# Two VectorE operands into PSUM, a reordered slot, and a convolution folded into TensorE's weights, in a two-layer Mamba and mixture-of-experts kernel

## What is computed

```
xz = xn @ in_proj.T ; x, z = split(xz)             # 256 channels each
xc = conv_b + sum over k of xp[:, k:k+L] * w[:, k] # 4 taps, causal, per channel
x = silu(xc)
delta = softplus(...) ; B, C from x                # 16 states per head
s[t] = s[t-1] * exp(delta * A) + delta * x * B     # the scan
y = sum over states of s * C ; y = (y + x * Dskip) * silu(z) ; out = y @ out_proj.T
# experts, every token through all eight:
h = silu(xn @ w_gate[e]) * (xn @ w_up[e]) ; g = sum over e of cw[e] * (h @ w_down[e])
```

## Time and profile before

| | us |
|---|---|
| median of 3 runs | 956.6 (956.46 to 961.53) |
| profiled execution | 957.64 |
| its span on the core | 955.8 |
| busy: PE, DVE, ACT, POOL | 827.9, 809.0, 427.4, 521.8 |
| start, up to the first layer 0 turn | 25.1 |
| layer 0, four turns | 400.6 |
| layer 1, three turns with the next pair's head | 400.2 |
| layer 1, last turn and end | 130.1 |

### The profile page before, as it was taken

The page is one execution under the profiler, slowest core; times in us unless marked ns, Lnnn a source line. Parts: engine busy times, 40 slices in busy tenths (PEclk is TensorE's granted clock), DMA queues, the critical chain, the costliest instruction groups (busy, mean ns, idle before and its releaser), DMA issues. The chain is left out here.

```text
span 955.8 us, 10838 instructions
## 1 busy us (share of the span) xinstructions
PE 827.9 (87%) x2368; PEld 403.0 (42%) x2368; DVE 809.0 (85%) x1127; ACT 427.4 (45%) x691; POOL 521.8 (55%) x336
## 2 busy tenths in 40 slices
PE   2947998899799979977799998899986999888997
PEld 1413443444344434333354443454443554444454
DVE  4389648956995698649999999999999999999995
ACT  2633455445445535455244633345553345533331
POOL 0067617652764365426654566654756455576773
PEclk9977999899899989889999999999999999999999
DMA  8253155313533255147554466565746544555861
GB/s 233 66 157 113 45 187 151 112 54 97 141 117 85 77 160 164 34 121 179 152 161 146 124 175 157 156 143 139 171 126 166 145 137 139 153 155 159 183 166 42
DMA packets 85275, 128.76 MB, mean 135 GB/s; under 512 B 7304, under 2 KB 27984, under 8 KB 85232
## 3 DMA queue, kind: packets, MB, share of 16 engines
q1 hardware_dynamic: 85232, 128.32, 49.6%
HBM read 124.82 MB, written 3.47 MB: 134 GB/s over the span
## 5 line engine op out<-in xcount | busy, mean ns | idle before, releaser
L880 POOL TENSOR_TENSOR product<-state,CB 128x512 f32<-128x512 f32 x128 | 203.6, 1592 | 193.4 <-DVE state L604 192.6
L604 DVE TENSOR_TENSOR_SCAN state<-decay,drive 128x512 f32<-128x512 f32 x192 | 274.0, 1429 | 5.0 <-ACT decay L1153 1.3
L1349 PE MATMUL bank<-XH,wh 128*128 128x512 f32 x256 | 193.1, 754 | 3.8 <-issue 2.0
L1153 ACT ACTIVATE decay<-delta,negA 128x510 f32<-128x510 f32 x192 | 135.5, 714 | 111.9 <-DVE state L604 111.6
L1463 PE MATMUL bank<-xw,wu 128*128 128x512 f32 x256 | 137.5, 619 | 51.0 <-DVE hid L734 50.3
L597 DVE TENSOR_TENSOR drive<-dx,CB 128x512 f32<-128x512 f32 x192 | 166.2, 867 | 9.4 <-DMA CB<-crow 6.2
L1411 PE MATMUL bank<-hid,wd 128*128 128x512 f32 x256 | 152.9, 681 | 9.5 <-ACT hid L1160 9.5
L1160 ACT ACTIVATE hid<-bank,early 128x512 f32<-128x512 f32 x128 | 87.3, 685 | 138.9 <-PE bank L1411 128.2
L1199 ACT ACTIVATE sg<-bank 128x512 f32<-128x512 f32 x128 | 75.9, 593 | 149.9 <-PE bank L1351 135.1
L1471 PE MATMUL bank<-hid,wd 128*128 128x512 f32 x256 | 133.2, 602 | 0.0
L1364 PE MATMUL bank<-product,early 128*128 128x512 f32 x232 | 117.2, 595 | 1.4 <-DVE xd L740 1.4
(11 more groups left out here) (158 smaller groups left out, 928.3 us busy)
## 6 DMA issues: line engine op xcount, KB each, us to landing
CB<-crow SPq DMA_DIRECT2D x256, 256.0 KB, 4.6
CB<-crow SPq DMA_DIRECT2D x64, 512.0 KB, 4.9
cwb<-cwrow SPq DMA_DIRECT2D x32, 256.0 KB, 5.8
wu<-W_dram SPq DMA_DIRECT2D x8, 256.0 KB, 5.8
wd<-W_dram SPq DMA_DIRECT2D x8, 256.0 KB, 6.6
wu<-Wu_dram SPq DMA_DIRECT2D x8, 256.0 KB, 4.1
xw<-Wg_dram SPq DMA_DIRECT2D x8, 256.0 KB, 4.3
wd<-Wd_dram SPq DMA_DIRECT2D x8, 256.0 KB, 4.9
```

The costliest lines, as they stand in the source:

```text
L604: v.tensor_tensor_scan(state[:, c % RING, :], decay[:, c % RING, :], drive[:, c % 2, :], 0.0, ALU.mult, ALU.add).then_inc(state_ready.sem, 1)
L880: ins = p.tensor_tensor(dst, state[:, c % RING, :], CB[:, c % ROWS, 0, :], ALU.mult)
L1153: a.activation(by_batch(decay[:, c % RING, :])[:, :, 1:], by_batch(delta[:, m, :])[:, :, 1:], ACT.Exp, scale=negA[:, c:c + 1]).then_inc(de ...
L1349: t.matmul(dst, wh[:, e, ws], XH[:, :], start=True, stop=False)
```

## The change

- PSUM: HIDS goes from 3 to 2, so two banks hold gate products (and layer 0's hidden units); one bank instead of two holds up products; the two banks gained hold dx (one buffer for both tiles) and drive (one buffer).
- VectorE's slot in layer 1 becomes: scan, hid, drive, gg. drive(c) waits for scan(c-1). dx of the second tile is formed by VectorE in slot 15, before that tile's first drive. In layer 0 the same single drive buffer stands with the old order, scan and then drive.
- TensorE's slot becomes: down(u-3), gate(u), late, up(u-1), sums, head. up(u-1) waits for hid(u-2), gate(u) for gg(u-2).
- The convolution of layer 1: at the start four rows of weights are loaded and multiplied into the input weights (`fold_conv`, GpSimd), and xi0 and xi1 become four accumulated products each, over tokens shifted by 0 to 3 in a padded XN (`XNP`). ScalarE's tanh and the halved convolution come straight from PSUM. The six taps on VectorE, the copy and the first tap on ScalarE go. The head steps are moved by some slots.
- The sum over chunks: GpSimd adds products in twos (16 more additions a turn, less the three of the first four) and TensorE adds 16 entries a turn instead of 29.

```diff
-HIDS = 3
+HIDS = 2
...
-HEAD1 = {6: "stat1", 7: "var1", 9: "xn", 11: "xnT", 12: "xi0", 13: "tap01 logits", 14: "lmax", 15: "tap02 lexp xi1",
-         16: "tap03 z0 tz0", 17: "th0 sz0", 18: "xs0", 19: "tap11", 20: "row0 tap12", 21: "z1 tz1 tap13 soft1", 22: "sz1 th1",
-         23: "xs1", 24: "dt0 soft2", 25: "row1 rest0 soft3", 26: "dt1 less0", 27: "cwT rest1", 28: "less1 ln", 29: "xr"}
+HEAD1 = {6: "stat1", 7: "var1", 9: "xn", 11: "xnT", 12: "xi0", 13: "logits", 14: "lmax", 15: "lexp",
+         16: "xs0 z0 tz0", 17: "sz0 xi1", 19: "xs1", 20: "row0", 21: "z1 tz1 soft1", 22: "sz1",
+         24: "dt0 soft2", 25: "row1 rest0 soft3", 26: "dt1 less0", 27: "cwT rest1", 28: "less1 ln", 29: "xr"}
...
+PAIR = 2
+ENTRIES = C1 // PAIR
+SUMS1 = [max(CHUNKS1[PAIR * e + PAIR - 1] + SUM_LAG1, LATE + 1) for e in range(ENTRIES)]
+SUMS1 = [max(at, CHUNKS1[N - 1] + SUM_LAG1 + 2) if PAIR * e >= N else at for e, at in enumerate(SUMS1)]
...
-        Y_BANK, OUT_BANK, HID_BANK, UP_BANK, HEAD_BANK = 0, 1, 2, 5, 7
+        Y_BANK, OUT_BANK, HID_BANK, DRIVE_BANK, UP_BANK, DX_BANK, HEAD_BANK = 0, 1, 2, 4, 5, 6, 7
...
+            for k in range(KC):
+                dst = w_cv[:, k, :] if k < KC - 1 else xw[:, 0, 0:J1 * 128]
+                sp.dma_start(dst, w["conv1"][k:k + 1, :].to_broadcast((128, J1 * 128))).then_inc(cv_in.sem, 16)
             for e in range(E):
                 load_wd(e, w["W2"][e])
...
-                dve.wait_ge(state_ready.sem, at(state_ready, max(c - 1, 0)))
-                v.tensor_tensor(drive[:, c % 2, :], dx[:, m, :], CB[:, c % ROWS, 1, :], ALU.mult).then_inc(drive_ready.sem, 1)
+                dve.wait_ge(state_ready.sem, at(state_ready, c))
+                v.tensor_tensor(drive, dx, CB[:, c % ROWS, 1, :], ALU.mult).then_inc(drive_ready.sem, 1)
...
+                for k, c in enumerate(now(CHUNKS1, u - 1)):
+                    if k > 0:
+                        form_drive(at, c, c // N, J1)
+                    scan(at, c)
                 if u >= 2:
                     finish_hidden(i, u - 2)
...
-                for c in now(CHUNKS1, u - 1):
-                    scan(at, c)
                 if u > 0:
-                    for c in now(CHUNKS1, u):
+                    for c in now(CHUNKS1, u)[:1]:
+                        if c == N:
+                            form_dx(at, 1, 1, N)
                         form_drive(at, c, c // N, J1)
...
+                e = c // PAIR
+                cs = CB[:, c % ROWS, 0, :]
+                if c % PAIR == 0:
+                    pool.wait_ge(summed.sem, at(summed, max(e - PRODS + 1, 0)))
+                    p.tensor_tensor(product[:, e % PRODS, :], state[:, c % RING, :], cs, ALU.mult).then_inc(state_used.sem, 1)
+                else:
+                    pool.wait_ge(group_ready.sem, at(group_ready, e))
+                    p.tensor_tensor(addend, state[:, c % RING, :], cs, ALU.mult).then_inc(state_used.sem, 1)
                     pool.wait_ge(state_used.sem, at(state_used, c + 1))
+                    p.tensor_tensor(product[:, e % PRODS, :], product[:, e % PRODS, :], addend, ALU.add).then_inc(group_ready.sem, 1)
...
+            def fold_conv():
+                pool.wait_ge(cv_in.sem, cv_in.at0(0, 16 * KC))
+                pool.wait_ge(late_in.sem, late_in.at0(0, 16 * 5))
+                w_x = w_in1[:, 0:J1 * 128]
+                for k in range(KC - 1):
+                    p.tensor_tensor(w_cv[:, k, :], w_cv[:, k, :], w_x, ALU.mult).then_inc(cv_step.sem, 1)
+                pool.wait_ge(cv_step.sem, cv_step.at0(0, KC - 1))
+                p.tensor_tensor(w_x, w_x, xw[:, 0, 0:J1 * 128], ALU.mult).then_inc(cv_ready.sem, 1)
...
                 if name in ("xi0", "xi1"):
                     act.wait_ge(*use1(head_ps, j, name))
+                    a.activation(th[:, :], hb[:, :], ACT.Tanh, bias=col1("bconv", m), scale=0.5).then_inc(th_ready.sem, 1)
+                    a.activation(conv[:, m, :], hb[:, :], ACT.Identity, bias=col1("bconv", m), scale=0.5).then_inc(head_read.sem, 1)
...
+                    for k in range(KC):
+                        taps = w_cv[:, k, :] if k < KC - 1 else w_in1[:, 0:J1 * 128]
+                        last = t.matmul(by_batch(hb[:, :]), taps[:, 128 * m:128 * m + 128], XNP[:, :, k:k + L], start=(k == 0), stop=(k == KC - 1))
...
-                pe.wait_ge(hid_ready.sem, hid_ready.at1(i, u - 1))
-                t.matmul(bank[UP_BANK + u % 2][:, :], wu[:, e, 128 * f:128 * f + 128], xw[:, e % 2, :], start=True, stop=True).then_inc(up_ps.sem, 1)
+                pe.wait_ge(hid_ready.sem, hid_ready.at1(i, u))
+                t.matmul(bank[UP_BANK][:, :], wu[:, e, 128 * f:128 * f + 128], xw[:, e % 2, :], start=True, stop=True).then_inc(up_ps.sem, 1)
...
+                if u > LAG1:
+                    down1(i, u - LAG1)
                 gate1(i, u)
+                if u > 0 and late:
+                    late(u)
+                if u == LAG1:
+                    down1(i, u - LAG1)
                 if u > 0:
                     up1(i, u - 1)
-                if u > 0 and late:
-                    late(u)
-                if u >= LAG1:
-                    down1(i, u - LAG1)
```

More of the change, by code:

```diff
@@ L241, in build @@
         hp = sb("hp", [128, TT])
-        delta, dx = sb("delta", [128, J1, T]), sb("dx", [128, J1, T])
+        delta = sb("delta", [128, J1, T])
+        dx = bank[DX_BANK][:, :]
         CB = sb("CB", [128, ROWS, 2, T])
         decay, state = sb("decay", [128, RING, T]), sb("state", [128, RING, T])
-        drive, product = sb("drive", [128, 2, T]), sb("product", [128, PRODS, T])
-        addend = product[:, PRODS - 1, :]
+        drive = bank[DRIVE_BANK][:, :]
+        product = sb("product", [128, PRODS + 1, T])
+        addend = product[:, PRODS, :]
         xd, szm = sb("xd", [128, J1, T]), sb("szm", [128, J1, T])
@@ L603, in scan @@
                 dve.wait_ge(state_used.sem, at(state_used, max(c - RING + 1, 0)))
-                v.tensor_tensor_scan(state[:, c % RING, :], decay[:, c % RING, :], drive[:, c % 2, :], 0.0,
+                v.tensor_tensor_scan(state[:, c % RING, :], decay[:, c % RING, :], drive, 0.0,
                                      ALU.mult, ALU.add).then_inc(state_ready.sem, 1)
@@ L733, in finish_hidden @@
                 dve.wait_ge(down_done.sem, down_done.at1(i, u - 1))
-                v.tensor_tensor(hid[:, u % 2, :], gg[:, u % 2, :], bank[UP_BANK + u % 2][:, :], ALU.mult).then_inc(hid_ready.sem, 1)
+                v.tensor_tensor(hid[:, u % 2, :], gg[:, u % 2, :], bank[UP_BANK][:, :], ALU.mult).then_inc(hid_ready.sem, 1)
             def finish_y(i, m):
-                dve.wait_ge(summed.sem, summed.at1(i, entry_of((m + 1) * N - 1) + 1))
+                dve.wait_ge(summed.sem, summed.at1(i, (m + 1) * N // PAIR))
                 dve.wait_ge(kept_ready.sem, kept_ready.at1(i, 1))
@@ L993, in _ @@
                     slot0(0, u - BEHIND, units=False)
+            fold_conv()
             with pool.Fori(0, PAIRS - 1) as i:
@@ L1286, in head_product @@
             def head_product(rows, weights, rhs):
-                t.matmul(hb[0:rows, :], weights, rhs, start=True, stop=True).then_inc(head_ps.sem, 1)
+                dst = hb[0:rows, :] if len(rhs.shape) == 2 else by_batch(hb[0:rows, :])
+                t.matmul(dst, weights, rhs, start=True, stop=True).then_inc(head_ps.sem, 1)
             def head0(name, j):
@@ L1331, in head1 @@
                         kind, tile = k // TT, k % TT
-                        last = t.matmul(hb[:, E * k:E * k + E], XNT[:, 128 * tile:128 * tile + 128],
+                        last = t.matmul(hb[:, E * k:E * k + E], xn_tile(tile),
                                         w_r1[:, E * kind:E * kind + E], start=True, stop=True)
@@ L1358, in sum_entry @@
                     pe.wait_ge(gated.sem, gated.at1(i, 0))
-                    pe.wait_ge(group_ready.sem, group_ready.at1(i, 1))
-                else:
-                    pe.wait_ge(state_used.sem, state_used.at1(i, c + 1))
-                if c == N:
+                if e == N // PAIR:
                     pe.wait_ge(yT_ready.sem, yT_ready.at1(i, 1))
-                t.matmul(bank[Y_BANK][:, :], ident[:, :], product[:, e % PRODS, :], start=(e == 0 or c == N), stop=(c % N == N - 1)).then_inc(summed.sem, 1)
+                pe.wait_ge(group_ready.sem, group_ready.at1(i, e + 1))
+                k = e % (N // PAIR)
+                t.matmul(bank[Y_BANK][:, :], ident[:, :], product[:, e % PRODS, :], start=(k == 0), stop=(k == N // PAIR - 1)).then_inc(summed.sem, 1)
             def sum_group(at, q):
```

99 lines of the change are left out of this document (42 added, 57 removed).

## The result

The changed kernel takes 965.4 us (median of 18 runs, 961.9 to 968.1), the kernel before in the same sessions 960.6 us (median of 18, 954.0 to 968.1). The ratio is 1.0061, 95% interval 1.004 to 1.0082: slower by 0.6%, where 954 and "slightly faster" were forecast. The profiled execution took 965.2 us, with a span of 963.4.

A forecast was written before the change was run, and what follows sets the result against it. VectorE was taken to bound layer 1, and some 44 us of each layer 0 turn, TensorE the rest. Terms -54.8 + 65 - 8 - 5 = -2.8 took 957.6 to 955, median 954 us; range 938 to 970.

The forecast's parts named there:

- the stalls of the one-bank loop: Layer 1: up waits for hid one slot later, so gg stalls behind uncovered products; +65 us, bounds 0 and 80.
- the -8 us for VectorE's other instructions: Layer 1: VectorE instructions still with two SBUF operands meet shorter GpSimd products; -8 us, between 0 and -20.
- layer 0's convolution: Layer 0's last turn: six more products of 0.86 us in the part that TensorE bounds.
- the operands in layer 0: Drive and dx in PSUM shorten ten scans and ten drives in VectorE's 44 us stretch; -3.6 us a turn.
- VectorE's work in layer 1: Taps -21.0, drive -24.8, scan -13.4, moved dx and pipeline gaps +4.4: together -54.8 us.
- The contention rival: PSUM operands do not spare scans and drives GpSimd's delays; 1008 us, about 980 if only one stays contended; chance 0.13.
- the sentence from the Trainium skill: VectorE: a PSUM source costs 120 cycles against 58 for SBUF, some 65 ns more an instruction; the prediction said the trace disagrees.
- The formula: Layer 1: gg stalls 0.04 + 0.86 us per product in the slot, less VectorE's extra work and gg's earlier stall.
- third rival: Layer 1: a TensorE wait in each turn brings 10 us at 1.2 GHz, 5 us lost a turn; 974 us, chance 0.08.
- Layer 0: All of layer 0: operands, last turn, hidden banks and start together give -5 us.
- The 4.8 us: Layer 0: with two hidden banks TensorE needs the rectified unit 1.2 us earlier, ScalarE late at the logarithm; 4 x 1.2 us.
- The rival that the loop does not bind: Layer 1: up, down and gate finish in time, so stalls vanish; 889 us, or 921 half hidden; chance 0.22.

The follow-up runs named there:

- e3: Changed kernel with TensorE's sums of layer 1 issued ahead of up instead of behind it: 949.5 us, ratio 0.990 to the kernel before.
- e9: Changed kernel with layer 1's convolution back on VectorE as taps: 949.9 us, ratio 0.987 to the kernel before.
- e10: Changed kernel with layer 1's products summed singly on TensorE, 29 entries a turn instead of 16: 985.8 us, ratio 1.027 to the kernel before.
- e1: Kernel before with only layer 0's dx and drive in PSUM and two hidden banks there, layer 1 unchanged: 927.6 us, ratio 0.967.
- e13: Kernel with layer 0 alone in PSUM (927.6 us), with one up bank in layer 1 and three gate banks kept: 959.5 us, ratio 1.000 to the kernel before.
- e12: Kernel with layer 0 alone in PSUM (927.6 us), with layer 1's drive in the third gate bank, dx in SBUF: 951.9 us, ratio 0.992 to the kernel before.

## Why the prediction was wrong

The steps that failed are three terms of the sum: the stalls of the one-bank loop, forecast at +65 us, came as +84; the -8 us for VectorE's other instructions came as some -2; and layer 0's convolution, priced at 5.2 us, cost 13. A fourth, the operands in layer 0, was short the other way and hid most of it. Term by term:

**VectorE's work in layer 1: right, but for the 8 us.** Forecast -54.8 and -8 us, measured -56.9. Scan and drive give 37.0 of it where 38.2 were forecast (drive 693 ns for 675, scan 1214 for 1227), the taps 21.0, and dx takes 3.0. That leaves some -2 for what else reads SBUF, of which -8 was expected: xn, delta and sp_e got shorter, xs and XL longer. The contention rival fell. So did the sentence from the Trainium skill (VectorE: DVE Perf Modes, TRN2 errata) for this pair: by the medians a source and destination in PSUM cost the drive 29 ns (693 for 664) and the scan nothing (1214 for 1216), not 65.

**The loop's stalls: right in kind, too small.** Forecast +65 us; VectorE's idle time grew by 84. The convolution's two stalls and the sums were placed right (e3, e9, e10). Before gg the three turns with a head wait 69 us where 53 were forecast, the last turn 11.1 for 11.7. Missed were the late hid with the clock's fall behind it, 3.67 us of stall where 0.9 was forecast and 0.71 for 0.4 in the next slot; the slot behind the first convolution, 2.06 for 0.85; and 8.2 us of waits before scans (1.0, 4.2, 2.9 and 0.1 in the four turns, of it 3.2 for one decay), of which the prediction has none. The formula takes VectorE's own work in a slot as cover for gg; an xn of 3.06 us, which stands ahead of hid in the new order, delays TensorE instead. The prediction's third rival asked for a wait "in each turn" that brings half clock, and priced it at 5 us a turn: that wait came, in addition to the forecast case rather than instead of it, and its two stalls stand 3 us above the forecast. The granted clock of layer 1's head turns is 0.95 to 0.96, 0.98 to 0.99 before.

**Layer 0: the larger miss.** Forecast -5, measured -19.4. Two terms failed in opposite directions. The operands were priced at 3.6 us a turn, less 4.8 us in all for the third hidden-layer bank, which makes -9.6; e1, which has exactly this part, shows -31.6, of it 11.4, 7.3, 5.9 and 7.0 us in the four turns. The 4.8 us did not come: TensorE's waits for the rectified unit in layer 0 are 9.5 us before and 8.1 in e1. The step counted ten scans and ten drives in a 44 us stretch; the whole turn has 16 of each, at 1673 and 830 ns, now 1217 and 698, which is 9.4 us. And TensorE's wait for xn shrank from 5.5 to 2.4 us, with the granted clock of the turn up from 0.93 to 0.98; the prediction named the shorter wait but priced neither. The convolution in the last turn was priced as six products of 0.86, 5.2 us; e9 shows 13: 2.4 more of waits, the one for sz among them, and some 5 of TensorE's work at a lower granted clock (0.91 for 0.97), which the prediction left out.

**The sum.** -62.8 + 65 - 5 = -2.8 was forecast; the spans give -56.9 + 83.9 - 19.4 = +7.6. Misses of +5.9, +18.9 and -14.4 us cancelled but for 10.4, so that the time was inside the range with the wrong sign. That it lies so near is luck.

**The rival that the loop does not bind** fell, by e13: one up bank alone costs 32 us. The account that VectorE and TensorE wait for each other through that bank was right. But the prediction took the order as given, to cover the gap between drive and scan. Its own arithmetic has the answer: with hid first VectorE needs 5.24 us from hid to gg(u+1), one scan more than 4.10, and a single product is then covered. Measured, the order cost 12 us.

**Best version.** Layer 0 in PSUM, layer 1 as before (e1): 927.6 us, 3.3% under the kernel before and 3.9% under the changed one. Parts that paid: the operands in layer 0, which has no up product, and by some 5 us the sums in twos with the operands in PSUM. Parts that did not: the same operands where they took the second up bank, the convolution, and the new order.

## What to carry to other kernels

A PSUM bank given to an elementwise operand is paid for where a matmul's output ring loses it: ask, stage by stage, what the ring's depth lets TensorE do ahead, and give the bank only in the stage where it lies idle. Here, work moved from VectorE to TensorE was worth nothing in a stage where both are near 90% busy (layer 1: 120.3 and 129.9 of 133.7 us), and cost 13 us for 5.2 us of products where TensorE is the bound. In a stream that is worked off in order, put work that is ready ahead of the instruction that waits, not behind it; that was worth 16 us with one up bank in the new order, under 4 in the old, and nothing with two banks, where up's wait is shorter (44.3 us for 89.3).

## What was not expected of the hardware

The scan and the drive of VectorE are held up beside GpSimd's products, which read two tensors from SBUF, when both their inputs lie in SBUF, and in e12's last turn the drive waits out the whole product. With one of the two inputs in PSUM, scans and drives kept within 1205 to 1222 and 684 to 700 ns over 192 executions, and GpSimd took 1274 in place of 1592. The Trainium skill (SBUF — State Buffer, section on who interferes with whom) has the rule: the pair of ports that the two share is an exclusive lock, held for the whole instruction, and a VectorE instruction with at most one SBUF input, outside the two-port modes, does not contend; for scan, drive, gg and hid the traces agree. One tensor input alone does not make an instruction safe: xn has one, and ranges from 332 to 1423 ns.

The loss can lock in. In e12's last turn a drive that starts 0.05 us behind a product, which the scan before it had released, takes 1.77 us, and so it goes in nearly every slot, 1671 ns on the mean, while the same drive took 802 in the turn 525.6 to 661.9, where head work shifts the two against each other. That turn of e12 takes 20.6 us more than e1's. Its scans are shorter (1208 ns on the mean for 1355) and its drives longer (1671 for 986), which together is 17.4 us.
